# Splitting a masking instruction by its rows, moving small sums from Pool to VectorE, and reordering the last steps of a fused attention and FP4 feed-forward kernel

## The reference

```python
q = elu(x @ Wq + bq) + 1;  k = elu(x @ Wk + bk) + 1;  v = x @ Wv + bv    # 16 heads of 16
k = k / sqrt(sum(k * k) + 1e-6)                                          # per head
attn = (q @ k.T) @ v                                                     # no softmax: linear attention
a = layernorm(x + attn @ Wo + bo, eps=1e-6) * gamma + beta
x1 = layernorm(x + a, eps=1e-5)
# feed-forward, all operands first quantised to FP4 (E2M1) in blocks of 16 and back
h = silu(Q(x1) @ Q(w_gate).T) * (Q(x1) @ Q(w_up).T)                      # 704 wide
out = layernorm(x1 + Q(h) @ Q(w_down).T, eps=1e-5)
```

## Time and profile before

| what | value |
|---|---|
| median of 3 runs | 689.85 us (688.17 to 692.0) |
| profiled execution | 687.63 us, span of its instructions 685.6 us |
| busy PE / PE weight load | 667.9 us (97%) / 584.8 us (85%) |
| busy DVE / ACT / POOL | 570.2 (83%) / 524.4 (76%) / 612.0 (89%) |
| granted TensorE clock, mean | 0.997 of full speed |

### The profile page before, as it was taken

The page is one execution under the profiler, slowest core; times in us unless marked ns, Lnnn a source line. Parts: engine busy times, 40 slices in busy tenths (PEclk is TensorE's granted clock), DMA queues, the critical chain, the costliest instruction groups (busy, mean ns, idle before and its releaser), DMA issues.

```text
span 685.6 us, 14440 instructions
## 1 busy us (share of the span) xinstructions
PE 667.9 (97%) x4216; PEld 584.8 (85%) x4216; DVE 570.2 (83%) x1438; ACT 524.4 (76%) x1037; POOL 612.0 (89%) x925
## 2 busy tenths in 40 slices
PE   7999999999999899999999999999999999999995
PEld 6888888888887789888989998999989989999994
DVE  5678778776779888899899999999988899988774
ACT  4677777775778667788888889888898888887663
POOL 3988898998979998898999999999999999998766
PEclk9999999999999999999999999999999999999998
DMA  8543344444311111444757555665557664500001
GB/s 271 193 139 132 120 134 130 139 139 154 124 63 32 34 60 47 95 96 97 143 116 160 129 128 115 124 163 131 126 98 119 112 145 95 110 17 16 32 17 46
DMA packets 51099, 74.39 MB, mean 109 GB/s; under 512 B 26380, under 2 KB 31054, under 8 KB 51022
## 3 DMA queue, kind: packets, MB, share of 16 engines
q1 hardware_dynamic: 50602, 73.35, 42.8%
q10 hardware_dynamic: 420, 0.13, 0.1%
HBM read 41.75 MB, written 25.89 MB: 99 GB/s over the span
## 4 chain that ended last, share of the span: by engine, by line
PE 69%; POOL 13%; issue 9%; DMA 3%; DVE 3%; ACT 2%; SPq 0%; POOLq 0%; DVEq 0%; ACTq 0%
PE banks L477 18%; PE banks L478 17%; PE banks L479 17%; PE banks L618 6%; POOL arena L1335 4%; PE banks L648 3%; POOL arena L1302 3%; PE banks L540 3%; DMA resid<-scales_scratch 2%; PE banks L488 2%; POOL arena L1305 1%; POOL lnbuf L1311 1%; PE banks L501 1%; POOL arena L1324 1%; DMA resid<-in_L_attn_Wv_dram 1%
## 5 line engine op out<-in xcount | busy, mean ns | idle before, releaser
L477 PE MATMUL banks<-wgu_hi,actT_lo 128*128 128x512 f32 (+1 forms) x384 | 145.5, 379 | 0.3 <-DVE actT_lo L1105 0.2
L478 PE MATMUL banks<-wgu_lo,actT_hi 128*128 128x512 f32 (+1 forms) x384 | 143.6, 374 | 0.0
L479 PE MATMUL banks<-wgu_hi,actT_hi 128*128 128x512 f32 (+1 forms) x384 | 143.2, 373 | 0.0
L477 PE MATMUL banks<-wd_hi,actT_lo 128*128 128x256 f32 x320 | 100.3, 313 | 0.1
L1302 POOL TENSOR_TENSOR arena<-arena 128x704 f32<-128x704 f32 x64 | 89.6, 1401 | 10.8 <-DVE arena L1090 10.8
L479 PE MATMUL banks<-wd_hi,actT_hi 128*128 128x256 f32 x320 | 90.3, 282 | 0.0
L478 PE MATMUL banks<-wd_lo,actT_hi 128*128 128x256 f32 x320 | 90.2, 282 | 0.0
L477 PEld LDWEIGHTS banks<-wgu_hi,actT_lo 128*128 128x128 f32 x384 | 72.4, 188 | 11.9 <-DVE actT_lo L1105 1.5
L479 PEld LDWEIGHTS banks<-wgu_hi,actT_hi 128*128 128x128 f32 x384 | 72.1, 188 | 10.5
L478 PEld LDWEIGHTS banks<-wgu_lo,actT_hi 128*128 128x128 f32 x384 | 72.4, 189 | 9.6
L1335 POOL TENSOR_TENSOR arena<-arena,s 128x960 f32<-128x960 f16 (+2 forms) x46 | 75.9, 1649 | 0.0
(11 more groups left out here) (146 smaller groups left out, 1966.3 us busy)
## 6 DMA issues: line engine op xcount, KB each, us to landing
xs<-x_plus_scratch SPq DMA_DIRECT2D x32, 512.0 KB, 4.2
x_plus_scratch<-xs SPq DMA_DIRECT2D x24, 512.0 KB, 2.9
resid<-scales_scratch SPq DMA_DIRECT2D x22, 512.0 KB
arena<-in_L_attn_x_dram SPq DMA_DIRECT2D x32, 256.0 KB, 3.6
out_dram<-arena SPq DMA_DIRECT2D x32, 256.0 KB, 6.1
x_plus_scratch<-arena SPq DMA_DIRECT2D x4, 512.0 KB, 2.9
x_plus_scratch<-resid SPq DMA_DIRECT2D x4, 512.0 KB, 3.4
resid<-in_L_attn_x_dram SPq DMA_DIRECT2D x4, 256.0 KB, 6.2
```

The costliest lines, as they stand in the source:

```text
L477: nc.tensor.matmul(dst, sl, mh, start=(k == 0), stop=False, skip_group_check=shared)
L478: nc.tensor.matmul(dst, sh, ml, start=False, stop=False, skip_group_check=shared)
L479: last = nc.tensor.matmul(dst, sh, mh, start=False, stop=(ended and k == n - 1), skip_group_check=shared)
```

## The change

There are three parts. First, for the 22 counts that are transposed by DMA, `cut` is two instructions: rows 13 to 15 (192 elements), then rows 0 to 12 (832 elements), which tells of the end. Second, for the steps 2 to 9 and 60 to 69 VectorE makes the two sums of `roots` (`root_sums(t + 1)`, behind the aggregates of step t), and Pool starts with the power. `roots(70)`, whose result nobody reads, is left out. Third, around T = 64: VectorE masks count 66 at the end of step 63 ahead of the scales of count 67, Pool dequantises count 66 in step 64 ahead of `over_scales(67)`, and from step 64 on ScalarE has `ln3_apply` behind `high_x` and `high_h`.

```diff
         ve, nm = (sb(n, [P, 3]) for n in ("ve", "nm"))
+        ve_dve, nm_dve = (sb(n, [P, 2, 3]) for n in ("ve_dve", "nm_dve"))
         rstd, nmr = (sb(n, [P, 2, 3]) for n in ("rstd", "nmr"))
...
 
+        SPLIT = 13
+
...
         vT_ps, x_hi_s, x_lo_s, h_hi_s, h_lo_s = (sem(n) for n in ("vT_ps", "x_hi", "x_lo", "h_hi", "h_lo"))
+        sums_s = sem("sums_by_dve")
         sT_ps, sT_s, sT_out, codes_in = (sem(n) for n in ("scales_turned", "scales_copied", "scales_out", "codes_in"))
...
+
+        SUMMED = [*range(2, 10), *range(60, LAST + 1)]
+
+        def summed(t):
+            return 2 * len([u for u in SUMMED if u <= t])
+
...
                     ln2_apply(t + 5, t)
-                if there(t - 6):
+                if there(t - 6) and t < T:
                     ln3_apply(t - 6, t)
...
+
+                if there(t - 6) and t >= T:
+                    ln3_apply(t - 6, t)
                 if there(t):
...
                 after(dve, deq_s, n - 1)
+                source, out = vqb[n % 2], lines(vqc[n % 2].bitcast(U16)[:, 0:VC * P])
+                b = b // RW
                 if by_dma(n):
-                    b = VC * P
-                nc.vector.tensor_scalar(lines(vqc[n % 2].bitcast(U16)[:, a:b]), vqb[n % 2][:, a // RW:b // RW, 0:RW],
-                                        ROUND_MASK, None, ALU.bitwise_and).then_inc(round_s, 1)
+
+                    nc.vector.tensor_scalar(out[:, SPLIT:, :], source[:, SPLIT:VC * P // RW, 0:RW], ROUND_MASK, None,
+                                            ALU.bitwise_and)
+                    b = SPLIT
+                nc.vector.tensor_scalar(out[:, a // RW:b, :], source[:, a // RW:b, 0:RW], ROUND_MASK, None,
+                                        ALU.bitwise_and).then_inc(round_s, 1)
 
...
 
+            def root_sums(t):
+                s = t % 2
+                dve.wait_ge(agg_s, aggregated(t - 1))
+                after(dve, root_s, rooted(t - 2))
+                nc.vector.tensor_tensor(ve_dve[:, s, :], mv[:, s, :, 1], eps_v[:, :], ALU.add).then_inc(sums_s, 1)
+                nc.vector.tensor_scalar(nm_dve[:, s, :], mv[:, s, :, 0], -1.0, None, ALU.mult).then_inc(sums_s, 1)
+
...
                     residual(t - 5)
-                if joint(t + 2):
+                if joint(t + 2) and t != T:
                     cut(t + 2)
...
                     aggregate(1, t, have + n3 + n1 + 1)
+                if t + 1 in SUMMED:
+                    root_sums(t + 1)
                 if there(t + 1) and t >= 0 and not late(t):
...
                     low_x(t + 1)
+                if t + 1 == T:
+                    cut(t + 3)
                 if joint(t + 4) and not pair(t + 33):
...
             def roots(t):
-                if t < FIRST + 2:
+                if t < FIRST + 2 or t > LAST:
                     return
                 s = t % 2
-                pool.wait_ge(agg_s, aggregated(t - 1))
+                if t not in SUMMED:
+                    pool.wait_ge(agg_s, aggregated(t - 1))
                 after(pool, z1_s, min(t + 6, T))
...
                 after(pool, root_s, rooted(t - 1))
-                nc.gpsimd.tensor_tensor(ve[:, :], mv[:, s, :, 1], eps_v[:, :], ALU.add).then_inc(ve_s, 1)
-                nc.gpsimd.tensor_tensor(nm[:, :], mv[:, s, :, 0], mone[:, :].broadcast_to([P, 3]), ALU.mult).then_inc(nm_s, 1)
-                pool.wait_ge(ve_s, rooted(t))
-                nc.gpsimd.tensor_tensor(rstd[:, s, :], ve[:, :], mhalf[:, :].broadcast_to([P, 3]), ALU.pow).then_inc(pow_s, 1)
+                if t in SUMMED:
+                    pool.wait_ge(sums_s, summed(t))
+                    sums, means = ve_dve[:, s, :], nm_dve[:, s, :]
+                else:
+                    sums, means = ve[:, :], nm[:, :]
+                    by_pool = rooted(t) - summed(t) // 2
+                    nc.gpsimd.tensor_tensor(sums, mv[:, s, :, 1], eps_v[:, :], ALU.add).then_inc(ve_s, 1)
+                    nc.gpsimd.tensor_tensor(means, mv[:, s, :, 0], mone[:, :].broadcast_to([P, 3]), ALU.mult).then_inc(nm_s, 1)
+                    pool.wait_ge(ve_s, by_pool)
+                    pool.wait_ge(nm_s, by_pool)
+                nc.gpsimd.tensor_tensor(rstd[:, s, :], sums, mhalf[:, :].broadcast_to([P, 3]), ALU.pow).then_inc(pow_s, 1)
                 pool.wait_ge(pow_s, rooted(t))
-                pool.wait_ge(nm_s, rooted(t))
-                nc.gpsimd.tensor_tensor(nmr[:, s, :], nm[:, :], rstd[:, s, :], ALU.mult).then_inc(root_s, 1)
+                nc.gpsimd.tensor_tensor(nmr[:, s, :], means, rstd[:, s, :], ALU.mult).then_inc(root_s, 1)
 
...
                     dequantise(t + 1)
+                if t == T:
+                    dequantise(t + 2)
                 if joint(t + 3):
...
                     ln1_affine(t + 7)
-                if joint(t + 2) and not SHIFT <= t < UNSHIFT:
+                if joint(t + 2) and not SHIFT <= t < UNSHIFT and t != T:
                     dequantise(t + 2)
...
```

## The result

| what | value |
|---|---|
| changed kernel, median of 6 runs | 696.21 us (693.37 to 697.55) |
| kernel before, median of 6 runs | 689.01 us |
| ratio | 1.0104, 95% interval 1.0079 to 1.0129 |
| profiled execution of the changed kernel | 693.37 us, span 691.3 us |

The change costs 7.2 us. One of the six runs of before took 945.59 us; without it the median is 688.17, and the change costs 8.0. The forecast was +2.5, and its range ended at 695.2, so the direction was right and the size was not. The profiled execution is the fastest of the six, so its span is only 5.7 us longer than that of before, and the other 1.5 us are not in it. The last experiment has a second profile of the same kernel.

A forecast was written before the change was run, and what follows sets the result against it. TensorE was taken as the bound, busy 667.9 of 685.6 us. Terms -2.0 (masks), +0.7 (middle), +0.3 (early sums), +3.5 (tail) gave +2.5, a median of 692.3 us; 8 in 10 range 687.2 to 695.2.

The forecast's parts named there:

- Masks in steps 10, 12, 14: Split masks no longer wait for Pool in these steps, so all 1.97 us come back: -2.0 us.
- Steps 1 to 3: VectorE's sums meet Pool and delay each step, partly offset by earlier roots: +0.3 us at the transposes of step 4.
- Steps 4 to 8: Gaps of 0.4 to 1.1 us on VectorE before line 1129 take in the sums' delay: no cost.
- The middle: Even steps from 16 to 54: the split mask delays `low_h`, so TensorE waits; +0.7 us, bounds 0 to 1.9.
- The tail: Sums waiting for Pool and the new order of the last steps together: +3.5 us (-0.4 to +4).
- Steps 59 to 66: Sums wait for Pool from step 61; slack covers step 62 (2.1 us late); count 65's transposes go 1.8 us late.
- With the sums: Last steps, new order and sums combined: transposes of count 66 are 2.1 us late, of count 67 3.5 us.
- rival A: The tiny sum doesn't wait for Pool and costs 0.26 us only in gaps: -2.0 us, 687.9 us; chance 0.22.
- The sum reads `mv` and `eps_v`, both in SBUF: VectorE's sum: two SBUF inputs need an exclusive lock, so it waits for Pool's running instruction.
- B: Steps 17 to 54: later masks move the transposing DMA onto Pool's path, +5 us more, 697 us; chance 0.07.
- C: Pool is freed more than counted and small waits in steps 16 to 54 go: -3.5 to -5, 685.5 us; chance 0.08.
- D: The split mask still waits, so the 2.0 us stay: +4.5, 694.4 us; chance 0.05.

The follow-up runs named there:

- The last experiment: The changed kernel run once more with nothing edited, for a second profile: 697.17 us, ratio 1.0106 against the kernel before.

## Why the prediction was wrong, point by point

**Masks in steps 10, 12, 14: right.** -2.0 us forecast, -2.0 measured, and -1.6 to -2.0 in the nine profiles that had the split there. Not all of it is the split's alone: with one-piece masks these steps lost 1.3 us with the moved wait alone and 0.7 with the sums alone, because fewer of the masks met Pool.

**Steps 1 to 3: right.** +0.3 forecast, +0.3 measured (steps 1 and 2 +1.1, steps 3 and 4 -0.8). "Steps 4 to 8: nothing" holds for the price, not for the reason. In step 5 the sum did meet Pool and took 1.76 us, and the gaps took that in (step 5: 8.37 us against 8.35).

**The middle: "I take less than half: +0.7 us" failed, in two ways.** By the table above the split from count 18 on costs some 1.5 us (1.8 to 3.3), within the bound of 0 to 1.9 that the prediction had worked out but twice the value it chose; the kernel with this alone measured +0.22% (-0.01 to +0.45). The mechanism that the prediction gave, TensorE waiting for a later `low_h`, is the one that the waits show. The larger part had no term at all. The moved wait leaves Pool idle for 0.144 us in each step, and the program at +0.24% alone (0.00 to +0.49), with 1.8 to 2.7 us in the table. The prediction read `roots` for what it moved to VectorE and not for the order of its waits, though the overlap was there to be read: two sums of 0.19 us, and yet 0.30 us from the first to the power.

**The tail: "+3.5" failed in size, through two of its steps.** It measured +4.9, and again +5.1 when the kernel was run once more. TensorE's transposes of counts 65, 66 and 67 were forecast 1.8, 2.1 and 3.5 us late. Counted from the start of step 60 they were 3.0, 4.8 and 4.9 late.

- "In sum 2.1 late, and `low_x` had 2.0 us of slack" and "Steps 59 to 66". The wait began in step 59, where the product and not the sum was caught (1.79 us). So steps 60 to 62 lost 1.5 us on TensorE that were forecast as nothing. In steps 61 and 62 TensorE stood for `low_x`, 0.58 and 0.36 us.
- "With the sums", the sum with the new order. Alone the order gains 0.34 us, as forecast (0.4), and the sums alone lose 3.8. Together they lose 4.9, 1.5 more than these two add up to. Step 64 shows where this comes from:

```profile
673.61 0.16 DVE L1164 TENSOR_TENSOR ve_dve<-mv,eps_v 128x3 f32<-128x3 f32 x1
673.63 1.39 POOL L1338 TENSOR_TENSOR arena<-arena 128x704 f32<-128x704 f32 x1
673.69 1.36 DVE L1165 TENSOR_SCALAR nm_dve<-mv 128x3 f32<-128x3 f32 x1
...
674.97 0.94 DVE L1130 TENSOR_TENSOR actT_lo<-banks,actT_hi 128x768 fp32r<-128x768 f32 x1
...
676.06 1.51 PE L658 MATMUL banks<-ident,arena 128*128 128x128 f32 x6 [3.08 <-DVE actT_lo L1130]
```

The order puts `over_scales(67)` behind the dequantising of 66. In the kernel with the order alone that is 1.3 us later than before (29.1 us after the start of step 60, not 27.8), and here it falls on the sums. The product waits for it, `low_h` starts 1.2 us late, and TensorE waits 3.08 us for it. In the kernel with the sums alone `over_scales` starts before the sums reach it, and the product starts as it ends:

```profile
672.34 1.39 POOL L1332 TENSOR_TENSOR arena<-arena 128x704 f32<-128x704 f32 x1 [1.58 <-DVE arena L1101]
...
673.69 0.16 DVE L1160 TENSOR_SCALAR nm_dve<-mv 128x3 f32<-128x3 f32 x1
```

**The clock, which had no term.** The slower clock adds 2.0 us to TensorE's busy time, but as far as the timeline shows it adds next to nothing to the tail of the changed kernel. From 676.06 TensorE works without a gap up to the transposes of count 67 at 680.08. The `low_h` that these need ended at 679.86, because it stood behind a sum that waited for Pool until 678.93. With the 0.15 us from one to the other that the prediction read the earlier trace rows, a TensorE at its upper level would have waited there until 680.0: an estimate of 0.1 us for the clock. In the kernel with the sums alone the same estimate gives up to 0.55 us of the 3.8, so the two causes don't add up exactly.

**The sum.** By the ratios of the parts alone: split -0.14%, moved wait +0.24%, sums +0.73%, order +0.12%, together +0.95% or 6.5 us, against the whole at 1.04 and 1.06%. Each has an interval of about 0.24% either way, so this agreement is worth some 3 us, no better.

**The reason for the port wait.** The mechanism was right: the tiny sum waits, and rival A (it doesn't) is out. What the prediction gave as the cause was wrong or at least not needed: "The sum reads `mv` and `eps_v`, both in SBUF". The sum with one input waits just as long, and the product with -1, which always had one input, took up to 1.79 us in the changed kernel. A sum with two inputs in another shape was not run, so two inputs may still be a reason of their own. What tells the cases apart is the shape. Four shapes were seen against a running Pool instruction:

| source, destination | waits for Pool | longest |
|---|---|---|
| 16 rows of 64, one run of 1024 | yes | 2.04 us |
| 15 rows of 64, one run of 960 | no | mean 0.64 us |
| 3 elements, 3 elements | yes | 1.79 us |
| 3 rows of 2, one run of 6 | no | 0.16 us |

The Trainium skill (Advanced Engine Details and Errata, 2x-2p Requirements) lets the two-port mode in when the outermost counts are both even, or odd, above one, and equal. If a wait for Pool is taken as the sign of that mode, and rows that touch count as one run, then by that rule the trace agrees in all four cases: 16 with 1024, and 3 with 3, are let in; 15 with 960, and 3 with 6, are not. The prediction took 15 rows for equal on both sides, though the destination has no gaps, and wrote "the rows show the opposite". Read in this way that was a misreading of the shape and no fault of the rule. Whether the engine merges touching rows itself was not tried.

**Rivals B, C and D.** B, the middle giving way through late codes, did not come about: SP waited for the mask 2.2 us in 6 places (before: 2.0 in 3), Pool waited less for the turned codes than before (6.1 us against 9.2), and the stalls are at `low_h`. In C the Pool of the middle was to be freed; the moved wait took more from it. D, a split mask that still waits, is excluded: the longest of the 22 pairs are 0.25 and 0.58 us.

**What stays open.** What each of the two causes costs in the middle is known to about 1 us only. The changed kernel's median loses about 1.5 us more than its first profile does. The second profile lies near the median and is 3.6 us longer than the first, mostly ahead of step 0, where the fourteen profiles lie up to 2.15 us apart whatever the edit. And whether sums in the tail are worth having once they are cheap: 0.9986 with them, 0.9972 and 0.9977 without, all within one another's intervals.

## What to carry to other kernels

Before work of Pool goes to VectorE, ask which shapes of instruction wait for Pool. In this kernel a three-element instruction was held until the Pool instruction that it met was over, and giving source and destination unequal counts (rows of two into one run) freed it. Price every line of a diff that moves a wait, even by two lines: ahead of an instruction that doesn't need the result, it costs the engine its overlap in each pass of the loop. Look first for the steps that have the stall, and edit there: with the mask cut in two for 3 of the 22 counts, and the new order, the kernel gained 0.2%; with the mask cut in two for all of them and nothing else it gained nothing that could be measured, though the intervals of these two overlap. And when TensorE's busy time grows with the same instructions, look at the granted clock, and then whether the longer work only fills a wait.

## What I had not expected of the hardware

- An instruction on three elements a partition, with one input, took 1.79 us beside Pool's `dequantise`, of which about 1.6 are the wait; two back to back can each wait, and the second can wait longer when the first slips through (0.16 and 1.79 in step 59).
- Twice the elements can be faster: 6 elements in 0.15 to 0.16 us always, 3 elements in 0.15 to 1.79.
- Pool waiting for its own last result ahead of the next instruction stands idle for 0.144 us (8.5 us in 59, 11.2 us in 78).
- Executions of one program differ in the middle by over 1 us and by where the stalls fall, while the steps at both ends repeat within 0.2 us.
- Behind waits of 1.21 and 3.08 us in the tail TensorE's granted clock fell to 1.2 GHz for 3.41 us, and yet the tail hardly got longer by it: the slower work filled a wait for VectorE.
